# Heads split in the heads loop, gate stores in whole transfers, and a first product between the two second blocks

## The chip, the cores and the metric

The kernel runs on one core of a Trainium2 chip. The metric is the device time of one execution in microseconds, lower being better. Times are medians over runs of the same kernel; the profile is of one execution.

## What is computed

Two "metaformer" stages over x of 32 images, 256 channels, 14 x 14 pixels. This change touches only the last sub-stage, a mixture of experts in which each of the 6272 tokens is cut into 8 heads of 32 values:

```python
h = x @ Wm + bm                       # tokens x 256
t = h.reshape(bs * L_ * H, HD)        # 8 heads of 32
w = jax.nn.softmax(t @ expert_emb, axis=-1)          # 16 experts
topw, topi = jax.lax.top_k(w, 2)
hmid = jax.nn.gelu(jnp.einsum('td,edi->tei', t, W1) + b1, approximate=False)
eo = jnp.einsum('tei,eio->teo', hmid, W2) + b2
comb = (take_along_axis(eo, topi) * topw[:, :, None]).sum(axis=1)
out = comb.reshape(bs, L_, d) @ Wo + bo              # added to the residual
```

The kernel computes all 16 experts for every head and weighs them with gates that are zero but for the top two.

## The kernel before

The program is a row of blocks; in each the five engines run their own instruction streams and meet at semaphores. Two blocks matter.

**The heads loop** (`T` = 16 chunks of `CH` = 392 tokens). Per chunk GpSimd gathers expert rows of an earlier stage (8 indirect DMAs, L1748), VectorE and ScalarE weigh them, normalise, squeeze and excite, and five steps after a chunk's weighing ScalarE's `heads` (L1909) writes the heads of the chunk into `hs`, a two-deep buffer. SP stores them to `hs_d` (L1715), and the exponentials of the gate logits to `ex_d` (L1717). `heads` waits until the store two chunks back has landed. The gates of a chunk ("route", 16 small VectorE steps, `route`, L1599 to L1622) need four transposes on TensorE (L1635), a copy to `wts` on VectorE (`route_copy`, L1643) and stores to `wt_d` on SP (`route_store`, L1649). Chunks 0 and 1 are routed at the end of the heads loop; the other 14 inside the expert loop. A store is one DMA for each of the 8 heads and each piece of the chunk that falls into one column of 256 tokens: 16 or 24 DMAs.

**The expert loop** runs over 49 units of 1024 columns (4 heads of 256 tokens; the last 8 heads of 128). SP loads a unit's heads four times, one below the other, into `stk` (L2158). GpSimd's `split` writes them as fp32r into `x_r` (L2206) and puts into rows 64 to 127 what the rounding lost (L2208). A unit is four slots, one for each group of four experts; the loop has 201 slots. In slot k TensorE does

- `first(4k+e)` for e = 0 to 3 (L2233): w1 times the unit, two matmuls of 512 columns into one of three `psA` buffers. It waits for the GELU three products back.
- after e=2, `second(k-1, b)` for b = 0 and 1 (L2243): w2 of four experts side by side on the columns of the array, into `psY`, which has two buffers.
- after e=0 the extras of the slot: `fold` (L2254, in slots 4w+6) adds up the four experts of a unit; `last` (L2264, in slots 8c+11 and 8c+12) is the output product; `route_pe` (L1635, 14 slots).

ScalarE does nothing but the GELU of each first product (L2292). VectorE runs in the same fixed order: the fold's copy (L2322), the output's sum (L2329), the copy to `wts`, then the two weighings with the gates (L2313), then the slot's route steps, if any. GpSimd adds the weighed groups (L2222). SP, in order, in slot k: the heads of the next unit every fourth slot, the exponentials of a later route, the gate stores, the gates of group k+2 (L2168, four DMAs of 128 KB, one for each expert, into one of three `wb` buffers), the output.

## Time and profile before

| | us |
|---|---|
| median of 3 runs (lowest, highest) | 2449.26 (2446.92, 2452.71) |
| the profiled execution, its own time | 2452.87 |
| its span on the chip | 2451.2 |

| engine | busy us | share |
|---|---|---|
| TensorE, matmuls | 2084.4 | 85% |
| VectorE | 1347.7 | 55% |
| ScalarE | 1289.6 | 53% |
| GpSimd | 968.5 | 40% |

The shares are means over blocks with different limits. The page names lines of the kernel (L2292) with the tiles they write and read; "[0.33 <-PE psA]" behind an instruction is the time for which its engine sat idle before it and what ended that.

### The profile page before, as it was taken

The page shows a single profiled execution, that of the slowest core. Times are in us where ns is not written, and L with a number is a line of the kernel's source. Part 1 is how long each engine was busy: PE and PEld are TensorE (multiplying, and loading weights), DVE is VectorE, ACT ScalarE, POOL GpSimd, SP SyncE. Part 2 cuts the span into 40 slices and gives each one's busy share as a digit, 9 for nine tenths or more (in the row PEclk, how much of TensorE's full clock was granted, in tenths as well). Part 3 has the DMA queues.
Part 4 walks back from the last instruction along what each step waited for, and adds up shares of the span by engine and source line. Part 5 has one row for each costly group of instructions (what it writes and reads, how often), then busy time and mean ns, then how long its engine had stood idle before and what let it go on. Part 6 is the DMA issues. An engine that isn't in the chain of part 4 may idle for free. (4 is left out here: it accounts for less than half of the span.)

```text
span 2451.2 us, 36445 instructions
## 1 busy us (share of the span) xinstructions
PE 2084.4 (85%) x12850; PEld 1158.6 (47%) x12851; DVE 1347.7 (55%) x2117; ACT 1289.6 (53%) x1634; POOL 968.5 (40%) x673
## 2 busy tenths in 40 slices
PE   6998599997977864775799964999999999999998
PEld 3444355554535544664466542444444444444444
DVE  5666435554458861221566652676666666666633
ACT  2444222222544421111344423888888888898887
POOL 4332111210004772001775002655565656565554
PEclk8999779998897757998698886999999999999999
DMA  2110212210724434555232104556565656565563
GB/s 54 28 33 8 86 46 68 65 64 34 250 62 126 145 98 129 172 172 158 72 106 93 48 33 104 141 143 156 147 172 146 156 149 160 148 159 145 146 157 107
DMA packets 206933, 274.84 MB, mean 112 GB/s; under 512 B 49190, under 2 KB 163446, under 8 KB 206646
## 3 DMA queue, kind: packets, MB, share of 16 engines
q1 hardware_dynamic: 173366, 227.84, 33.6%
q0 software_dynamic: 12288, 25.72, 3.5%
q10 hardware_dynamic: 21120, 19.18, 2.3%
q8 instruction: 98, 1.61, 0.3%
q14 instruction: 61, 0.50, 0.1%
HBM read 203.76 MB, written 68.83 MB: 111 GB/s over the span
## 5 line engine op out<-in xcount | busy, mean ns | idle before, releaser
L2292 ACT ACTIVATE BIG<-psA,b_s 128x1024 f32<-128x1024 f32 x784 | 809.8, 1115 | 127.8 <-PE psA L2233 127.5
L2233 PE MATMUL psA<-x_r,w_r 128*128 128x512 f32 x1568 | 477.9, 427 | 46.8 <-ACT BIG L2292 24.9
L2222 POOL TENSOR_TENSOR BIG<-BIG 128x1024 f32<-128x1024 f32 x147 | 376.6, 2562 | 356.4 <-DVE BIG L2313 222.6
L2313 DVE SCALAR_TENSOR_TENSOR BIG<-psY,b_s,BIG 128x512 f32<-128x512 f32 x392 | 292.1, 750 | 340.4 <-PE psY L2243 261.6
L2233 PEld LDWEIGHTS psA<-x_r,w_r 128*128 128x128 f32 x1568 | 269.3, 190 | 314.5 <-ACT BIG L2292 220.9
L2243 PE MATMUL psY<-BIG,w_s 128*32 128x512 f32 x3136 | 388.0, 607 | 15.9 <-DVE BIG L2313 8.2
L2243 PEld LDWEIGHTS psY<-BIG,w_s 128*32 128x32 f32 x3136 | 80.1, 109 | 214.8 <-issue 132.2
L715 DVE TENSOR_REDUCE b_nm<-psN 112x32 f32<-112x512 f32 x128 | 83.1, 686 | 152.9 <-PE psN L612 152.5
L1191 POOL DMA_INDIRECT xg_d<-xnb,SLOT x128 | 135.0, 1055 | 80.4 <-DVE SLOT L1306 43.9
L1524 PE MATMUL ps<-BIG,xv 128*128 x528 | 132.4, 394 | 39.2 <-ACT xv L1535 29.5
L1748 POOL DMA_INDIRECT gath<-yg_d,SLOT x128 | 137.2, 1072 | 65.8 <-issue 36.9
L553 POOL CAST b_pat_r<-BIG 72x3584 fp32r<-72x3584 f32 x16 | 50.7, 3170 | 224.8 <-PE psN L612 211.9
L1535 ACT ACTIVATE xv<-ps 128x512 f32<-128x512 f32 x66 | 39.4, 597 | 188.9 <-PE ps L1513 188.9
L715 DVE TENSOR_REDUCE a_nm<-psN 98x32 f32<-98x512 f32 x128 | 82.4, 685 | 89.0 <-PE psN L603 88.9
L1524 PEld LDWEIGHTS ps<-BIG,xv 128*128 128x128 f32 x528 | 95.8, 191 | 65.0 <-issue 54.5
L2206 POOL CAST x_r<-xv 128x1024 fp32r<-128x1024 f32 x49 | 51.9, 1059 | 186.8 <-DMA xv<-hs_d 186.6
L2208 POOL TENSOR_TENSOR x_r<-xv,x_r 64x1024 fp32r<-64x1024 f32 x49 | 118.0, 2407 | 3.9
L576 PE MATMUL ps<-BIG,b_wb 72*128 72x392 f32 x256 | 100.6, 539 | 3.5 <-DVE xv L721 3.5
L771 ACT ACTIVATE b_exs<-ps 128x1568 f32<-128x1568 f32 x32 | 47.3, 1477 | 104.3 <-PE ps L581 104.3
L1733 POOL MEMSET embd<- 128x64 f32 x1 | 0.2, 156 | 211.9 <-POOLq L1496 211.9
L612 PE MATMUL psN<-b_wb_r,b_pat_r 73*112 73x128 f32 x512 | 71.1, 286 | 14.8 <-POOL b_pat_r L553 14.0
L612 PEld LDWEIGHTS psN<-b_wb_r,b_pat_r 73*112 73x112 f32 x512 | 61.5, 194 | 35.6 <-POOL b_pat_r L553 14.8
(394 smaller groups left out, 3266.3 us busy)
## 6 DMA issues: line engine op xcount, KB each, us to landing
BIG<-wt_d SPq DMA_DIRECT2D x784, 128.0 KB, 2.8
xv<-hs_d SPq DMA_DIRECT2D x196, 128.0 KB, 3.0
BIG<-ypad_d SPq DMA_DIRECT2D x144, 120.0 KB
xg_d<-ex SPq DMA_DIRECT2D x64, 264.0 KB, 3.8
xv<-xg_d SPq DMA_DIRECT2D x66, 256.0 KB, 2.9
xv<-x SPq DMA_DIRECT2D x64, 196.0 KB, 2.7
yg_d<-ex ACTq DMA_DIRECT2D x33, 256.0 KB, 3.2
yg_d<-sq ACTq DMA_DIRECT2D x33, 256.0 KB, 3.2
```

Source lines behind the costliest of these rows:

```text
L576: eng.matmul(ps4[:, i, 0:CH], w_, src, start=True, stop=False)
L612: mm = eng.matmul(psN[0:SR, bank, g * 128:(g + 1) * 128], pat_r[0:KR, bank * 4 + g, sub * SR:(sub + 1) * SR], wb_r[0:KR, bank * 4 + g], st ...
L715: eng.tensor_reduce(dst, src, AX.X, ALU.max, negate=True).then_inc(S["max"], 1)
L1191: eng.indirect_dma_start(xg_d.ap(), bass.IndirectOffsetOnAxis(ap=SLOT[:, t * NSUB + s, j:j + 1], axis=0), xnb[:, t % XB, s], None).then_in ...
L1524: m = eng.matmul(psZ[:, u, r * C:(r + 1) * C], xt[:, u, r, h * 128:(h + 1) * 128], w_moe_s[:, bass.ds(e * (2 * C) + h * C, C)], start=(h = ...
L1748: eng.indirect_dma_start(gath[:, c % GB, 2 * s + j], None, yg_d.ap(), bass.IndirectOffsetOnAxis(ap=SLOT[:, c * NSUB + s, j:j + 1], axis=0) ...
L2208: eng.tensor_tensor(x_r[64:128, w % 2], stk[64:128, w % 2], x_r[64:128, w % 2].bitcast(F32), ALU.subtract).then_inc(Q["lo"], 1)
L2222: eng.tensor_tensor(gacc[:, w % 2], gacc[:, w % 2], gsum[:, a % 2], ALU.add).then_inc(Q["acc"], 1)
L2233: mm = eng.matmul(psA[m % 3][:, b * BLK:(b + 1) * BLK], w1_r[:, m % 16], x_r[:, w % 2, b * BLK:(b + 1) * BLK], start=True, stop=True)
L2243: mm = eng.matmul(psY[use % 2][32 * e:32 * e + 32, :], w2_s[:, g % 4 * 4 + e], hid[:, (4 * g + e) % 8, b * BLK:(b + 1) * BLK], start=True, ...
L2292: eng.activation(hid[:, m % 8], psA[m % 3][:], ACT.Gelu, bias=b1_s[:, m % 16:m % 16 + 1]).then_inc(Q["gel"], 1)
L2313: eng.scalar_tensor_tensor(out=dst, in0=psY[use % 2][:], scalar=b2_s[:, g % 4:g % 4 + 1], in1=wb[:, g % 3, b * BLK:(b + 1) * BLK], op0=ALU ...
```

## The change

Four things change.

1. GpSimd splits the heads in the heads loop, once per chunk and eight chunks behind the gathers: into `hs_r`, in the memory of `xs`. SP stores both parts, two DMAs per chunk, into `hs_d`, now of two planes. In the expert loop SP loads both straight into `x_r`; `split` and `stk` are gone.
2. `wt_d` is laid out as column, head, expert, token instead of expert, column, head, token. A gate store is then one DMA of all 128 rows for each piece: 2 or 3 of them. A gates load reads 4 heads of one expert, 16 KB apart, in pieces of 1 KB instead of 4 KB in one.
3. `fold` moves from behind e=0 to just before the second blocks, and is last of the extras in order.
4. In slots whose extras are none or a fold alone, the second block b=1 follows first product e=3 instead of standing behind b=0.

```diff
-                for h in range(NH):
-                    eng.dma_start(wt_d.ap()[:, c, h, at_:at_ + n], wts[h * NE:(h + 1) * NE, off:off + n]).then_inc(q_wst, 16)
+                eng.dma_start(wt_d.ap()[c].rearrange("h e n -> (h e) n")[:, at_:at_ + n], wts[:, off:off + n]).then_inc(q_wst, 16)
...
-        hs_d = nc.dram_tensor("hs_d", [C, T * CH], F32)
-        wt_d = nc.dram_tensor("wt_d", [NE, -(-(T * CH) // 256), NH, 256], F32)
+        hs_d = nc.dram_tensor("hs_d", [2, C, T * CH], F32)
+        wt_d = nc.dram_tensor("wt_d", [-(-(T * CH) // 256), NH, NE, 256], F32)
...
-                    wait(eng, H["hs"], c + 1)
-                    eng.dma_start(hs_d.ap().rearrange("(h p) (t c) -> t p h c", h=2, t=T)[c], hs[:, c % 2]).then_inc(f_hst[c % 2], 16)
+                    wait(eng, H["lo"], c + 1)
+                    for i in range(2):
+                        eng.dma_start(hs_d.ap()[i].rearrange("(h p) (t c) -> t p h c", h=2, t=T)[c], hs_r[:, i].bitcast(F32)).then_inc(f_hst, 16)
...
+                def split(c):
+                    wait(eng, H["hs"], c + 1)
+
+                    wait(eng, f_hst, c * 32)
+                    eng.tensor_copy(hs_r[:, 0], hs[:, c % 2]).then_inc(H["hi"], 1)
+                    wait(eng, H["hi"], c + 1)
+                    eng.tensor_tensor(hs_r[:, 1], hs[:, c % 2], hs_r[:, 0].bitcast(F32), ALU.subtract).then_inc(H["lo"], 1)
+
+                LEAD = 8
+                for c in range(T + LEAD):
+                    if live(c):
+                        gather(c)
+                    if live(c - LEAD):
+                        split(c - LEAD)
...
                 def heads(c):
-                    wait(eng, f_hst[c % 2], c // 2 * 16)
+                    wait(eng, H["lo"], c - 1)
...
-            EXTRAS[k] = [kind for kind, table in (("fold", FOLD), ("last", LAST), ("route", ROUTE)) if k in table]
+            EXTRAS[k] = [kind for kind, table in (("last", LAST), ("route", ROUTE), ("fold", FOLD)) if k in table]
...
         def heads_load(eng, w):
-            wait(eng, Q["lo"], w - 1)
+            wait(eng, Q["mm1"], 16 * (w - 1))
             tok, n, head, heads = UNITS[w]
             for r in range(4):
-                eng.dma_start(stk[32 * r:32 * r + 32, w % 2, 0:heads * n].rearrange("p (q c) -> p q c", q=heads),
-                              hs_d.ap()[32 * head:32 * (head + heads), tok:tok + n].rearrange(
+                eng.dma_start(x_r[32 * r:32 * r + 32, w % 2, 0:heads * n].bitcast(F32).rearrange("p (q c) -> p q c", q=heads),
+                              hs_d.ap()[r // 2, 32 * head:32 * (head + heads), tok:tok + n].rearrange(
                                   "(q p) c -> p q c", q=heads)).then_inc(q_stk[w % 2], 16)
...
-                src = wt_d.ap()[g % 4 * 4 + e, tok // UT, head:head + heads, 0:n]
+                src = wt_d.ap()[tok // UT, head:head + heads, g % 4 * 4 + e, 0:n]
...
                         if k < NG:
                             first(4 * k + e)
-                        if e == 0 and "fold" in EXTRAS[k]:
-                            fold(FOLD[k], EXTRA_USE["fold", k])
                         if e == 0 and "last" in EXTRAS[k]:
                             last(*LAST[k], EXTRA_USE["last", k])
                         if e == 0 and "route" in EXTRAS[k]:
                             route_pe(eng, ROUTE[k], EXTRA_USE["route", k])
-                        if e == 2 and 0 < k <= NG:
-                            for b in range(NB):
+                        if e == 2 and "fold" in EXTRAS[k]:
+                            fold(FOLD[k], EXTRA_USE["fold", k])
+                        for b in range(NB if 0 < k <= NG else 0):
+                            if e == (2 + b if EXTRAS[k] in ([], ["fold"]) else 2):
                                 second(k - 1, b)
```

## Rows read from the trace of the kernel before

**Rows 1.** Busy time by engine in the expert loop: PE, PEld, DVE, ACT, POOL, clock, DMA.
```profile
1510.00:2440.00 930.00, 889.34 (x5319) 397.77 (x5318) 573.80 (x723) 809.45 (x784) 537.58 (x242) 0.99 0.57 150
```

**Rows 2.** ScalarE's timeline: start us, us, GELUs of one slot, idle before them.
```profile
1569.43 4.13 ACT L2292 ACTIVATE BIG<-psA,b_s 128x1024 f32<-128x1024 f32 x4 [1.70 <-PE psA L2233]
1573.89 4.13 ACT L2292 ACTIVATE BIG<-psA,b_s 128x1024 f32<-128x1024 f32 x4 [0.34 <-PE psA L2233]
1578.62 4.13 ACT L2292 ACTIVATE BIG<-psA,b_s 128x1024 f32<-128x1024 f32 x4 [0.60 <-PE psA L2233]
```

**Rows 3.** Timeline, TensorE in slots without an extra: start us, us.
```profile
1966.44 0.73 PE L2233 MATMUL psA<-x_r,w_r 128*128 128x512 f32 x2 [0.27 <-ACT BIG L2292]
1967.10 1.92 PE L2243 MATMUL psY<-BIG,w_s 128*32 128x512 f32 x16
1967.56 0.13 PEld L2243 LDWEIGHTS psY<-BIG,w_s 128*32 128x32 f32 x4 [0.30 <-ACT BIG L2292]
1967.99 0.13 PEld L2243 LDWEIGHTS psY<-BIG,w_s 128*32 128x32 f32 x4 [0.30 <-issue]
1968.96 1.67 PE L2233 MATMUL psA<-x_r,w_r 128*128 128x512 f32 x6
```

**Rows 4.** Timeline, TensorE in a slot with an output product.
```profile
2433.65 1.20 PE L2233 MATMUL psA<-x_r,w_r 128*128 128x512 f32 x4
2434.69 1.02 PE L2264 MATMUL psY<-ex,wo_s 128*128 128x256 f32 x4
2435.37 1.28 PE L2233 MATMUL psA<-x_r,w_r 128*128 128x512 f32 x4
2436.58 1.92 PE L2243 MATMUL psY<-BIG,w_s 128*32 128x512 f32 x16
```

**Rows 5.** Timeline, a gate store of 24 DMAs and what follows.
```profile
1645.10 11.25 SPq L1649 DMA_DIRECT2D wt_d<-wts  x24
1656.45 1.76 SPq L2168 DMA_DIRECT2D BIG<-wt_d  x4
1665.77 3.12 ACT L2292 ACTIVATE BIG<-psA,b_s 128x1024 f32<-128x1024 f32 x3 [3.65 <-PE psA L2233]
```

**Rows 6.** Timeline, from the heads loop into the expert loop.
```profile
1479.80 20.25 SPq L1649 DMA_DIRECT2D wt_d<-wts  x40
1486.32 0.92 PE L1635 MATMUL ps<-ident,BIG 98*128 98x98 f32 x4 [9.02 <-DVE BIG L1622]
1488.22 0.57 DVE L1643 COPY wts<-ps 128x392 f32<-128x392 f32 x1 [1.96 <-DMA wt_d<-wts]
1501.50 1.75 SPq L2158 DMA_DIRECT2D xv<-hs_d  x4
1510.37 7.14 ACT L2292 ACTIVATE BIG<-psA,b_s 128x1024 f32<-128x1024 f32 x7 [7.58 <-PE psA L2233]
1512.60 0.50 PEld L2233 LDWEIGHTS psA<-x_r,w_r 128*128 128x128 f32 x2 [0.43 <-DMA wo_s<-wo]
```

**Rows 7.** DMA issues of the whole program: KB each, median us to landing.
```profile
BIG<-wt_d SPq DMA_DIRECT2D x784, 128.0 KB, 2.8
xv<-hs_d SPq DMA_DIRECT2D x196, 128.0 KB, 3.0
```

**Rows 8.** Single lines in the expert loop: duration ns min/median/max, first and last start.
```profile
L1606 DVE TENSOR_TENSOR rt<-rt,rev x28: 674/682/2864, 1531.5 to 2299.8; 98x512 f32<-98x512 f32 x28
L2206 POOL CAST x_r<-xv x49: 1026/1037/1500, 1505.6 to 2410.7; 128x1024 fp32r<-128x1024 f32 x49
L2208 POOL TENSOR_TENSOR x_r<-xv,x_r x49: 2336/2386/2843, 1506.7 to 2411.8; 64x1024 fp32r<-64x1024 f32 x49
```

**Rows 9.** Timeline of the heads loop: VectorE, GpSimd and TensorE around a chunk's gathers.
```profile
1321.31 1.66 DVE L1757 SCALAR_TENSOR_TENSOR yn<-gath,P,yn 98x256 f32<-98x256 f32 x4
1323.81 0.96 POOL L1748 DMA_INDIRECT gath<-yg_d,SLOT  x1 [4.06 <-DVE yn L1757]
1324.21 0.79 PEld L1965 LDWEIGHTS psN<-ident,yn 98*128 98x128 f32 x8
```

More of the change, by code:

```diff
@@ L1064, in build @@
         yg_d = nc.dram_tensor("yg_d", [TILES * ROWS, C], F32)
-        Q = {k: sem(f"q_{k}") for k in ("w", "wo", "set", "hi", "lo", "mm1", "gel", "put", "got", "acc", "rt")}
+        Q = {k: sem(f"q_{k}") for k in ("w", "wo", "set", "hi", "mm1", "gel", "put", "got", "acc", "rt")}
         q_wst = sem("q_wst")
@@ L1579, in stored_gates @@
         def stored_gates(r):
-            return 16 * NH * sum(len(s) for s in GATE_STORES[:r])
+            return 16 * sum(len(s) for s in GATE_STORES[:r])
         def gates_ps(use):
@@ L1647, in route_store @@
             for c, at_, off, n in GATE_STORES[r]:
-                for h in range(NH):
-                    eng.dma_start(wt_d.ap()[:, c, h, at_:at_ + n], wts[h * NE:(h + 1) * NE, off:off + n]).then_inc(q_wst, 16)
+                eng.dma_start(wt_d.ap()[c].rearrange("h e n -> (h e) n")[:, at_:at_ + n], wts[:, off:off + n]).then_inc(q_wst, 16)
         H = {k: sem(f"h_{k}") for k in ("w", "set", "scl", "w0", "y", "tr", "x2", "mean1", "dev1", "sq1", "var1", "log1", "rstd1", "n1",
                                         "ys", "gate", "max", "gexp", "hid", "div", "gtr", "gt", "bc", "mul", "w2", "sgx", "sig", "x3",
-                                        "mean2", "dev2", "sq2", "var2", "log2", "rstd2", "n2", "lin", "hs", "lgd", "mx", "dl", "exp")}
+                                        "mean2", "dev2", "sq2", "var2", "log2", "rstd2", "n2", "lin", "hs", "hi", "lo", "lgd", "mx", "dl", "exp")}
         GB = 3
         h_g = [sem(f"h_g{b}") for b in range(GB)]
-        f_hst = [sem(f"f_hst{u}") for u in range(2)]
+        f_hst = sem("f_hst")
         f_wst = [sem(f"f_wst{u}") for u in range(2)]
-        hs_d = nc.dram_tensor("hs_d", [C, T * CH], F32)
-        wt_d = nc.dram_tensor("wt_d", [NE, -(-(T * CH) // 256), NH, 256], F32)
+        hs_d = nc.dram_tensor("hs_d", [2, C, T * CH], F32)
+        wt_d = nc.dram_tensor("wt_d", [-(-(T * CH) // 256), NH, NE, 256], F32)
         ex_d = nc.dram_tensor("ex_d", [T, SUB, NSUB * NH * NE], F32)
@@ L1683, in build @@
         hs = BIG[:, 2 * T * CH:2 * T * CH + 4 * CH].rearrange("p (u h c) -> p u h c", u=2, h=2)
+        hs_r = xs.bitcast(F32R)
         sq2, rs2 = ex, at[:, 0]
@@ L1724, in _ @@
                         route_store(eng, 0, 0)
+                eng.wait_ge(f_hst, T * 32)
                 for u in range(2):
-                    eng.wait_ge(f_hst[u], T // 2 * 16)
                     eng.wait_ge(f_wst[u], T // 2 * 16)
@@ L1742, in _, with gather @@
                                       base=-32 * r, pattern=[[-1, HD]], channel_multiplier=1).then_inc(Q["set"], 1)
-                for c in range(T):
+                def gather(c):
                     wait(eng, H["w0"], c - GB + 1)
@@ L2095, in build @@
         fin = BIG[:, 30 * BLK:30 * BLK + 2 * UT].rearrange("p (a c) -> p a c", a=2)
-        stk = xv[:].rearrange("p a u h c -> p (a u h c)")[:, 0:4 * BLK].rearrange("p (a c) -> p a c", a=2)
         comb = ex[:].rearrange("p h c -> p (h c)")[:, 0:2 * UT].rearrange("p (a c) -> p a c", a=2)
@@ L2200, in _ @@
             def _(eng):
-                def split(w):
-                    wait(eng, q_stk[w % 2], (w // 2 + 1) * 64)
-                    wait(eng, Q["mm1"], 16 * (w - 1))
-                    eng.tensor_copy(x_r[:, w % 2], stk[:, w % 2]).then_inc(Q["hi"], 1)
-                    wait(eng, Q["hi"], w + 4)
-                    eng.tensor_tensor(x_r[64:128, w % 2], stk[64:128, w % 2], x_r[64:128, w % 2].bitcast(F32),
-                                      ALU.subtract).then_inc(Q["lo"], 1)
-                    wait(eng, Q["lo"], w + 1)
-                split(0)
                 for w in range(NU):
-                    if w + 1 < NU:
-                        split(w + 1)
                     for g in range(1, 4):
@@ L2228, in first @@
                     if m % 16 == 0:
-                        wait(eng, Q["lo"], w + 1)
+                        wait(eng, q_stk[w % 2], (w // 2 + 1) * 64)
                     wait(eng, Q["gel"], m - 2)
@@ L2332, in _ @@
                 for k in range(SLOTS):
-                    if "fold" in EXTRAS[k]:
-                        combine(FOLD[k], EXTRA_USE["fold", k])
                     if "last" in EXTRAS[k]:
@@ L2338, in _ @@
                         route_copy(eng, ROUTE[k], EXTRA_USE["route", k])
+                    if "fold" in EXTRAS[k]:
+                        combine(FOLD[k], EXTRA_USE["fold", k])
                     for b in range(NB if 0 < k <= NG else 0):
```

## The prediction

> **What bounds the kernel now.** I read the page first: its chain of work that ended last goes back only to the start of the last block, the expert loop. So the busy times of that stretch came next [rows 1]. It is 930 us of 2451, with TensorE busy for 889 us, ScalarE for 809, VectorE for 574, GpSimd for 538 and the DMA engines for 57% of it, at a granted clock of 0.99. The stage is 809 us of GELU plus ScalarE's idle time, so each microsecond of that idle time that goes is a microsecond of the whole.
>
> ScalarE's own timeline says where it idles [rows 2]. Four GELUs take 4.13 us, and ahead of the last one of each slot there is one gap: 0.33 us in slots without an extra (such a slot lasts 4.46 us), 0.55 to 1.0 with a fold (48 slots, mean 0.67), about 0.65 with an output product (4.78 us), and 1.70 in every sixth output slot (seven in all). Four slots show 3.3 to 3.8 us.
>
> The small gaps come from TensorE's order [rows 3]. After the first product e=2 stand both second blocks, 1.86 us; only then comes e=3, for which ScalarE is already waiting. In the slot without extra TensorE itself idles 0.27 us, for a GELU, ahead of e=2. In the output slot [rows 4] TensorE's parts add up to the slot itself, 4.78 us: there its work is the bound.
>
> The large gaps come from SP's queue [rows 5]: 24 gate stores hold it for 11.25 us, the gates loads behind them start at 1656.45, and ScalarE stands still for 3.65 us before 1665.77.
>
> Last the seam ahead of the loop [rows 6]. 40 gate stores occupy SP for 20.25 us, to 1500.05, although the last gates are in `wts` at 1488.8. The loads of the heads start at 1501.50, GpSimd splits them, and the first GELU starts at 1510.37, after 7.58 us of waiting for TensorE.
>
> **Gate stores.** Each store issue costs SP about 0.5 us (20.25/40; 11.25/24 = 0.47). Ahead of the loop 40 become 5. The two of chunk 0 leave at 1479.8 and have landed long before 1487. Then VectorE's copy is late: the transposes end at 1487.24 [rows 6], the copy (0.57, now held 1.96 us by a store's landing) at 1487.9; three stores end by 1489.3. From SP's last store to the first load of the loop there are now 1.45 us, so this load goes at 1490.75 instead of 1501.50: **-10.7 us**. In the loop 16 or 24 issues become 2 or 3, and the queue is held for 1.4 us at most. The four large gaps (slots 32, 80, 128, 152; the first is in rows 5) shrink to 0.33: 14.4-1.3 = 13.1 us; three of about 1 us after other stores give 2: **-15 us**.
>
> The new layout makes a gates load 1 KB pieces instead of 4 KB. Heads loads already move 128 KB in 1 KB pieces, in 3.0 us against 2.8 for a 4 KB gates load [rows 7]. Gates have two slots of lead and DMA is busy 57%, so I take 0. The bounds are 0 and, were each group's load in the open, 0.2 x 196 = 39 us.
>
> **Split moved into the heads loop.** In the loop it removes a cast and a subtraction of GpSimd, 1.04 and 2.39 us [rows 8], per unit; only the first pair lies open, 3.5 us after the landing. TensorE could start that much sooner, but its second slot waits for `wo_s`, which lands at 1512.6 [rows 6] and moves only with the seam. Its product is there 1.1 us later, at 1513.7, and the fifth GELU, now at 1510.37+4x1.03 = 1514.5, starts then: **-0.8 us** (bounds 0 and 3.5). It also ends GpSimd's reads in the slots ahead of each fold: a route step takes up to 2.9 us beside GpSimd's two-input work and 0.68 by itself [rows 8].
>
> In the heads loop each chunk gets a CAST and a subtraction of 784 columns instead of 1024: 1.04 x 784/1024 = 0.8 and 2.39 x 784/1024 = 1.8 us, and one store more (some 0.4 us of an SP that idles most of the time). GpSimd now ends a chunk's gathers at 1319.75 and waits 4.06 us for VectorE [rows 9]; 2.6 us fit. The store's landing, awaited by the next split, is hidden by a whole chunk, and `heads` waits for a split two chunks back. But GpSimd's subtraction would stand beside VectorE's L1757, two inputs from SBUF, at 1321.3. Delayed to the subtraction's end (1322.8) it ends at 1324.4 instead of 1322.97; TensorE wants it from 1324.21: 0.2 to 0.3 us in each of the eight chunks that still gather. Later GpSimd is idle and splits as soon as the heads are there, when nothing long with two inputs runs. The last split ends some 3 us after the last heads, before the `exp` that SP waits for anyway. Bounds 0 and 16 x 1.8 = 29 us; I take **+1 us**, since the cover is seen in the rows.
>
> The Trainium skill ("SBUF — State Buffer", section Who interferes with whom) says that a VectorE instruction with two SBUF inputs and a GpSimd instruction that reads SBUF block each other wholly. The trace agrees: 0.68 to 2.86 us for one and the same step [rows 8]. By this rule the price is the subtraction's full length wherever both meet, 29 us were all of it on the path; that is the upper bound above.
>
> **First product between the second blocks.** TensorE's terms [rows 3]: one matmul of a first product in a row costs (1.67-0.73)/4 = 0.235 us; a first product from a standstill until the next second block 0.66; two second blocks 1.86, which are four turns of 0.43 (weight loads at 1967.56 and 1967.99) and 0.14 until the first product can start. Parted they pay that 0.14 twice: 2.00. (No row has a block between two first products; 0 and the whole 0.43 of another turn are the bounds.) A split slot is then: e=0, 1, 2 in a row 0.66+4x0.235 = 1.60; e=3 alone 0.66; blocks 2.00: **4.26 us** against 4.46. GELU needs 4.13, so TensorE is the bound, and e=3 is ready about 0.5 us ahead of its GELU. A fold beside the blocks adds two turns of half the columns, 0.43: 4.69 against 4.73 to 4.83, mean 4.80, so -0.11. Two output slots of eight keep their order. Their terms now [rows 4]: two first products ahead of the output product 1.04, that 0.68, e=1 and 2 1.21, blocks 1.86, sum 4.79. The first loses its leading e=3 to the slot before (1.04-0.47 = 0.57) and is 4.32; the second stays 4.79; the slot after them runs e=3, 0, 1 and waits for the GELU as now (4.46-0.66-1.86 = 1.94), then 0.66, both parted blocks 2.00 and e=3 0.66, in all 5.26. The three are 14.37 against 4.78+4.78+4.46 = 14.02. Over eight slots: 3 x -0.20, 2 x -0.11, +0.35, which is -0.47. Times 24.5 (-11.5), less seven slots that have a route and stay as they are (1.4): **-10 us**.
>
> What is queued behind: `fold` and its copy stand later in the slot, and the second block b=1 waits for the copy. With a route step of 0.7 us ahead, the copy ends 0.6 us before b=1 is due. The seven gaps of 1.70 stay: there two route steps, one of them long, hold up VectorE before the output's sum.
>
> The Trainium skill ("TensorEngine Tiling (Array Packing)", Key Properties) says that a change of tiling mode drains TensorE; this change makes four such changes a slot out of two. The rows put 0.14 us on the way back to a first product; the rule names no price.
>
> **Sum.** -10.7 - 15 - 0.8 + 1 - 10 = -35.5 us. The profiled execution took 2452.87 us (span 2451.2 and 1.7 around it), 3.6 above the median 2449.26. I take the sum from the median, 2413.8, and say **2413 us**.
>
> **The rivals.**
> A: parting the blocks costs more than 0.14, say 0.25 us. 141 slots are split; 141 x 0.11 = 16: 2429. (Were it 0.14+0.43, another turn lost each time, it would be 61: 2474.) For it: no row shows a block between two first products without a wait near it. Chance 0.15.
> B: the restart is hidden and slots run at the GELU rate, 0.13 less in 141 slots: 2395. Against it: a lone first product takes 0.66 where two in a row take 0.47. Chance 0.15.
> C: VectorE becomes late. The second weighing follows 0.9 us later, the route steps after it, and fold slots wait for the copy 0.5 us in 48 slots: 2437. For it: VectorE runs beside GpSimd's additions in three slots of four. Chance 0.07.
> D: the large gaps come from the stores' landings, not their issues, and stay: 2428. Against it: in rows 5 the gates load follows the last store's issue at once. Chance 0.04.
> E, slower: in the heads loop each split lies on the path, since GpSimd's next gathers start after it and VectorE is blocked by it: 2.65 us a chunk, 16 x 2.65 = 42: 2455. From 36/16 = 2.3 us a chunk on the kernel is slower. The 4.06 us of idle GpSimd speak against it. Chance 0.04.
>
> **How the numbers follow.** The forecast holds 2403 to 2422, chance 0.55. The range takes in A, B and D: 2392 to 2432; outside are C, E, A's far end and the tails. Less than 0.2% (4.9 us, about what a measurement of this kernel tells from no change) needs nearly all gains to fall away at once: same 0.02, slower 0.04, faster 0.94.
>
> **What would show it.** Seam: SP has 5 store issues, and the loop's first heads load starts some 11 us sooner after the last `ex_d` store. Store gaps: no wait of ScalarE above 1.8 us in the loop. Order: slots without extra 4.2 to 4.3 us; at 4.13 it is B, at 4.37 and over A. Heads loop: GpSimd waiting about 1.3 us a chunk instead of 4.06, and no later end. Wrong if the gates loads land later than the weighing wants them, or the clock of the expert loop falls below 0.98.

## The result, and the profile after

The changed kernel takes **2428.87 us** (median of 4 runs, 2427.95 to 2433.28) against 2448.09 for the kernel before, measured beside it (4 runs, 2446.78 to 2452.71): a ratio of 0.992 with a 95% interval of 0.9903 to 0.9936. It is faster by 19 us and inside the range of 2392 to 2432, but 16 us above the forecast of 2413 and outside 2403 to 2422. The profiled execution took 2433.28 us, with a span of 2431.6.

I cut both traces at the same events: the first weighing on ScalarE (L1872 before, L1888 after), the start of the last write of `heads` (L1909, L1925), SP's first load of the expert loop, the first GELU and the start of the last one.

| us | before | after | difference | forecast |
|---|---|---|---|---|
| blocks ahead of the heads loop (not touched) | 1163.3 | 1168.4 | +5.1 | 0 |
| heads loop | 311.8 | 319.5 | **+7.7** | +1 |
| seam: last heads to first load | 26.4 | 15.8 | **-10.6** | -10.7 |
| first load to first GELU | 8.9 | 5.6 | -3.3 | -3.5 |
| first GELU to last GELU | 928.8 | 909.8 | **-19.1** | -22.3 |
| rest | 12.0 | 12.5 | +0.6 | 0 |
| span | 2451.2 | 2431.6 | -19.6 | -35.5 |

The forecasts of the two rows around the first GELU are the sum's -15, -10 and -0.8 (-25.8), of which 3.5 lie ahead of it. Most of what is missing is in the heads loop and ahead of it.

The expert loop in the busy times by window (window, its length, then PE, PEld, DVE, ACT, POOL, granted clock, DMA share, GB/s), which answers [rows 1]:

```profile
1510.00:2420.00 910.00, 892.17 (x5317) 386.84 (x5315) 524.87 (x724) 811.67 (x784) 373.21 (x146) 0.99 0.57 154
```

All 784 GELUs now fit into 910 us. TensorE's timeline answers [rows 3] and [rows 4], one slot below the other:

```profile
1960.92 1.67 PE L2233 MATMUL psA<-x_r,w_r 128*128 128x512 f32 x6
1962.53 1.06 PE L2243 MATMUL psY<-BIG,w_s 128*32 128x512 f32 x8
1963.52 0.73 PE L2233 MATMUL psA<-x_r,w_r 128*128 128x512 f32 x2
1964.18 1.06 PE L2243 MATMUL psY<-BIG,w_s 128*32 128x512 f32 x8
1965.18 1.67 PE L2233 MATMUL psA<-x_r,w_r 128*128 128x512 f32 x6
1966.78 0.64 PE L2254 MATMUL psY<-BIG,fold 128*32 128x256 f32 x8
1967.23 1.04 PE L2243 MATMUL psY<-BIG,w_s 128*32 128x512 f32 x8
1968.20 0.73 PE L2233 MATMUL psA<-x_r,w_r 128*128 128x512 f32 x2
1968.87 1.06 PE L2243 MATMUL psY<-BIG,w_s 128*32 128x512 f32 x8
1969.87 0.73 PE L2233 MATMUL psA<-x_r,w_r 128*128 128x512 f32 x2
```

The slot without an extra runs from 1960.92 to 1965.18, 4.26 us, and the one with a fold from there to 1969.87, 4.69 us. Nothing stands idle in either. ScalarE's timeline answers [rows 2] and [rows 5]. The first row shows the gap of 1.70 that stays; the second is the place of the first large store gap (slot 32), now 16 GELUs without a gap that the view would part:

```profile
1571.92 5.13 ACT L2292 ACTIVATE BIG<-psA,b_s 128x1024 f32<-128x1024 f32 x5 [1.70 <-PE psA L2233]
1655.82 16.89 ACT L2292 ACTIVATE BIG<-psA,b_s 128x1024 f32<-128x1024 f32 x16 [0.56 <-PE psA L2233]
```

SP's timeline of the same store, the timeline of the seam (answers [rows 6]), and the DMA issues (KB each, median us to landing; answer [rows 7]):

```profile
1646.47 1.38 SPq L1648 DMA_DIRECT2D wt_d<-wts  x3
1647.95 1.81 SPq L2183 DMA_DIRECT2D BIG<-wt_d  x4
...
1500.07 0.57 DVE L1643 COPY wts<-ps 128x392 f32<-128x392 f32 x1 [1.01 <-PE ps L1635]
1503.67 1.76 SPq L2173 DMA_DIRECT2D x_r<-hs_d  x4
1509.29 4.13 ACT L2292 ACTIVATE BIG<-psA,b_s 128x1024 f32<-128x1024 f32 x4 [4.33 <-PE psA L2233]
1515.39 2.93 PE L2233 MATMUL psA<-x_r,w_r 128*128 128x512 f32 x6 [3.58 <-DMA wo_s<-wo]
1516.65 2.12 ACT L2292 ACTIVATE BIG<-psA,b_s 128x1024 f32<-128x1024 f32 x2 [3.24 <-PE psA L2233]
...
BIG<-wt_d SPq DMA_DIRECT2D x784, 128.0 KB, 3.2
x_r<-hs_d SPq DMA_DIRECT2D x196, 128.0 KB, 3.5
```

Three store issues hold SP for 1.38 us instead of 11.25. In the kernel before, VectorE's weighing waited 16 times for a gates load (us in total, times, longest, from 1520 to 2430 us); in the changed kernel the same view has no wait of L2313 for a DMA:

```profile
DVE BIG L2313 <- DMA BIG<-wt_d: 57.5, 16, 6.8
```

In the seam the first load goes 3.6 us after VectorE's copy starts. But the four GELUs that now start early are followed by a wait of 3.24 us: TensorE's slot 1 waits for `wo_s`.

The heads loop, in the timeline around one chunk, answers [rows 9]:

```profile
1282.42 4.44 DVE L1773 SCALAR_TENSOR_TENSOR yn<-gath,P,yn 98x256 f32<-98x256 f32 x4
1283.73 0.85 POOL L1756 CAST xv<-BIG 128x784 fp32r<-128x784 f32 x1
1284.67 1.91 POOL L1758 TENSOR_TENSOR xv<-BIG,xv 128x784 fp32r<-128x784 f32 x1
1286.91 0.56 PE L1981 MATMUL psN<-ident,yn 98*128 98x98 f32 x4 [0.96 <-DVE yn L1773]
```

The four weighing instructions take 4.44 us instead of 1.66. The difference, 2.78, is GpSimd's cast and subtraction together (0.85+1.91 = 2.76), and TensorE waits for VectorE. Six of the 16 groups are over 2 us (4.44, 3.84, 2.25, 4.45, 2.24, 2.24), which adds up to the 9.5 us that the loop's rows differ by. Over the whole loop (VectorE's groups by line in the stretch of the heads loop: busy us, mean ns), before and then after:

```profile
L1757 DVE SCALAR_TENSOR_TENSOR yn<-gath,P,yn 98x256 f32<-98x256 f32 x64 | 26.6, 478 | 11.8 <-ACT yn L1872 11.8
```

```profile
L1773 DVE SCALAR_TENSOR_TENSOR yn<-gath,P,yn 98x256 f32<-98x256 f32 x64 | 36.1, 625 | 12.1 <-ACT yn L1888 12.1
```

### The profile page after: what moved, and what is told of

Read it like the earlier page. It is cut to its first block and busy times, and to the rows that moved or that the text cites. A ratio compares the mean times of both kernels' runs of the same rounds, so it can differ in the third digit from the quotient of the medians.

```text
span 2431.6 us, 36080 instructions
## 1 busy us (share of the span) xinstructions
PE 2097.1 (86%) x12850; PEld 1151.0 (47%) x12851; DVE 1312.8 (54%) x2117; ACT 1292.7 (53%) x1634; POOL 847.6 (35%) x607
## 5 line engine op out<-in xcount | busy, mean ns | idle before, releaser
L2233 PE MATMUL psA<-x_r,w_r 128*128 128x512 f32 x1568 | 484.7, 428 | 19.8 <-ACT BIG L2292 8.2
L2313 DVE SCALAR_TENSOR_TENSOR BIG<-psY,b_s,BIG 128x512 f32<-128x512 f32 x392 | 292.9, 750 | 341.7 <-PE psY L2243 341.3
L2243 PE MATMUL psY<-BIG,w_s 128*32 128x512 f32 x3136 | 407.4, 603 | 6.2 <-DVE BIG L2329 5.9
L2243 PEld LDWEIGHTS psY<-BIG,w_s 128*32 128x32 f32 x3136 | 71.8, 108 | 155.5 <-issue 88.8
L1550 DVE COPY ex<-ps 128x512 f32<-128x512 f32 x33 | 22.8, 691 | 95.7 <-PE ps L1524 94.0
L791 ACT ACTIVATE BIG<-psMO 128x196 f32<-128x196 f32 x32 | 10.7, 333 | 109.6 <-PE psMO L636 109.6
```

The costliest lines, as they stand in the source:

```text
L2233: mm = eng.matmul(psA[m % 3][:, b * BLK:(b + 1) * BLK], w1_r[:, m % 16], x_r[:, w % 2, b * BLK:(b + 1) * BLK], start=True, stop=True)
L2243: mm = eng.matmul(psY[use % 2][32 * e:32 * e + 32, :], w2_s[:, g % 4 * 4 + e], hid[:, (4 * g + e) % 8, b * BLK:(b + 1) * BLK], start=True, ...
L2313: eng.scalar_tensor_tensor(out=dst, in0=psY[use % 2][:], scalar=b2_s[:, g % 4:g % 4 + 1], in1=wb[:, g % 3, b * BLK:(b + 1) * BLK], op0=ALU ...
```

## The experiments

All times are medians; "loop" is the stretch from the first to the last GELU. Ratios are to the kernel before, measured beside each of three groups (its medians there: 2451.67, 2450.18 and 2448.32 us), so kernels of different groups are compared by their ratios.

| kernel | us | ratio (95%) | heads loop | loop |
|---|---|---|---|---|
| blocks together | 2444.39 | 0.9971 (0.9953 to 0.9990) | 318.8 | 924.0 |
| stores by head | 2468.28 | 1.0065 (1.0048 to 1.0082) | 319.6 | 935.8 |
| split among the gathers | 2440.88 | 0.9951 (0.9926 to 0.9976) | 332.9 | 909.7 |
| split in the expert loop | 2426.13 | 0.9900 (0.9882 to 0.9918) | 313.1 | 908.9 |
| output weight later | 2426.98 | 0.9908 (0.9891 to 0.9925) | 320.0 | 904.7 |
| no split | 2421.48 | 0.9888 (0.9872 to 0.9903) | 309.4 | 909.1 |
| split off GpSimd | 2439.23 | 0.9958 (0.9944 to 0.9971) | 322.9 | 909.0 |
| changed kernel again | 2431.71 | 0.9922 (0.9908 to 0.9935) | 319.7 | 910.0 |
| split behind the weighing | 2423.35 | 0.9901 (0.9886 to 0.9917) | 316.3 | 910.0 |
| the same, output weight later | 2419.97 | 0.9890 (0.9875 to 0.9905) | 315.6 | 904.6 |
| split in the expert loop, output weight later | 2422.56 | 0.9892 (0.9877 to 0.9908) | 312.3 | 908.1 |
| order alone | 2442.86 | 0.9987 (0.9971 to 1.0003) | 310.9 | 916.7 |

**1. Blocks together.** The changed kernel with one condition changed:

```diff
-                            if e == (2 + b if EXTRAS[k] in ([], ["fold"]) else 2):
+                            if e == 2:
                                 second(k - 1, b)
```

> The changed kernel, with both second blocks behind e=2 in every slot (the fold still right before them); all else as changed. My theory: a split slot lasts 4.25 us and one with both blocks together 4.46, a fold slot 4.7 against 4.8, and the slot after two output slots gives 0.35 back, so the order is worth 0.35 to 0.5 us in eight slots: 8 to 12 us, time 2437 to 2441, slots without extra back at 4.46. Rival: the whole gain of the expert loop (22 us) is the missing store stalls, and the order is worth nothing: 2429. Other rival: the order is worth 20 us or more and something else in the loop lost: 2449.

The loop is 924.0 us against 909.8: parting the blocks is worth 14.3 us here, more than the 10 of the sum. Some 1.3 of it falls in the first three slots; the rest is 1.5 us for each 24 slots (from slot 86 to slot 110 this kernel needs 112.96 us and the changed one 111.42). A part of it is the fold: with its new place directly ahead of both blocks it makes a gap of 0.76 us at ScalarE (at 1819.54), in all 47 fold slots behind the start, where the kernel before had 0.67 on average. That is some 4 us (47 x 0.09) which the kernel before did not pay, so I estimate the parting at about 10 against that kernel. Rival A falls.

**2. Stores by head.** The changed kernel, its layout kept, with one DMA for each head again:

```diff
-                eng.dma_start(wt_d.ap()[c].rearrange("h e n -> (h e) n")[:, at_:at_ + n], wts[:, off:off + n]).then_inc(q_wst, 16)
+                for h in range(NH):
+                    eng.dma_start(wt_d.ap()[c, h, :, at_:at_ + n], wts[h * NE:(h + 1) * NE, off:off + n]).then_inc(q_wst, 16)
```

> The changed kernel with the new layout of the gates and loads in 1 KB pieces, but stored head by head again: 40 store DMAs ahead of the expert loop and 16 or 24 in it. My theory: it is the issues that cost, so the seam grows by 10.6 us, four gaps of ScalarE over 3 us come back and cost 13 to 15 us: 2429 + 24 to 26 = 2453 to 2455. Rival (D): the landing of the stores, or the layout, made the gaps: then only the seam comes back, 2440.

The seam is 12.0 us longer (27.8) where I expected 10.6, and the loop 26.0 us where I expected 13 to 15: the median is 13 us above the upper end of the forecast for this kernel, and above the kernel before. Rival D falls: the layout is the changed kernel's, and SP, which waits for the stores' landing ahead of the gates loads, does so for 0.4 us at most (us in total, times, longest):

```profile
SPq L2184 <- DMA wt_d<-wts: 5.8, 14, 0.4
```

The kernel before waits as little (5.7 us, 14 times, 0.4). Slot 32 in the timeline:

```profile
1666.15 1.80 SPq L2184 DMA_DIRECT2D BIG<-wt_d  x4
1671.27 1.41 DVE L2314 SCALAR_TENSOR_TENSOR BIG<-psY,b_s,BIG 128x512 f32<-128x512 f32 x2 [6.93 <-DMA BIG<-wt_d]
1675.30 1.11 ACT L2293 ACTIVATE BIG<-psA,b_s 128x1024 f32<-128x1024 f32 x1 [3.90 <-PE psA L2234]
1678.27 2.12 ACT L2293 ACTIVATE BIG<-psA,b_s 128x1024 f32<-128x1024 f32 x2 [1.85 <-PE psA L2234]
```

ScalarE stands still for 5.75 us. From SP's issue of the gates to VectorE's use of them it takes 5.12 us; in the kernel before it was 4.16 (the issue at 1656.45 in [rows 5]):

```profile
1660.61 1.41 DVE L2313 SCALAR_TENSOR_TENSOR BIG<-psY,b_s,BIG 128x512 f32<-128x512 f32 x2 [6.70 <-DMA BIG<-wt_d]
```

**3. Order alone.** To see whether that is the price of the order, the kernel before got only the new order of slots:

```diff
-                        if e == 0 and "fold" in EXTRAS[k]:
-                            fold(FOLD[k], EXTRA_USE["fold", k])
...
-                        if e == 2 and 0 < k <= NG:
-                            for b in range(NB):
+                        if e == 2 and "fold" in EXTRAS[k]:
+                            fold(FOLD[k], EXTRA_USE["fold", k])
+                        for b in range(NB if 0 < k <= NG else 0):
+                            if e == (2 + b if EXTRAS[k] in ([], ["fold"]) else 2):
                                 second(k - 1, b)
```

> The kernel before with the new order of slots alone; stores head by head, split in the expert loop. Theory from the two halves measured so far (the changed kernel without whole stores has a GELU stretch of 935.8 us): with 24 stores in a row SyncE issues the gates' loads late, and more slots stall than before, so the order alone brings nothing: GELU stretch 930 to 937 us, time 2449 to 2456 us. Rival (the order's gain of 14.3 us is its own and does not need the stores): 2435 to 2440 us.

My theory fell, and the median, 2442.86, lies between its forecast and the rival's. The loop is 916.7 us, 12.2 shorter than before, with the 24 stores in place; its first GELU, though, comes 1.5 us later behind the first load. The profiled span is 10 us shorter, the median 5.5, and the interval of the ratio takes in 1: by the medians alone the order by itself isn't told from no change, and its worth is read from the loop. Slot 32 again, SP, VectorE and ScalarE:

```profile
1657.00 1.76 SPq L2168 DMA_DIRECT2D BIG<-wt_d  x4
1661.12 1.41 DVE L2313 SCALAR_TENSOR_TENSOR BIG<-psY,b_s,BIG 128x512 f32<-128x512 f32 x2 [5.80 <-DMA BIG<-wt_d]
1663.78 1.11 ACT L2292 ACTIVATE BIG<-psA,b_s 128x1024 f32<-128x1024 f32 x1 [1.41 <-PE psA L2233]
```

The gates are as late as in the kernel before, but ScalarE waits 2.0 us at this place (1.41 and, one GELU later, 0.60) instead of 3.65: with e=3 between the blocks it has one more GELU to do while b=1 waits for VectorE. So order and stores overlap: 12.2 us for the order alone and 26.0 for the stores on top of the changed kernel are not terms of one sum. The kernel of experiment 2 differs from this one also in a later landing (median 3.4 us for a gates load against 2.8) and a longer issue (12.30 us for 24 stores against 11.38). That these two make it so much worse is argued from the rows; no run has them apart. Which of the layout and the second half of `hs_d` brings the later landing stands in the next experiment's DMA rows.

**4. Split in the expert loop.** The kernel before with whole stores, new layout and new order, so the changed kernel less its first part (two of the places, against the changed kernel):

```diff
-                    for i in range(2):
-                        eng.dma_start(hs_d.ap()[i].rearrange("(h p) (t c) -> t p h c", h=2, t=T)[c], hs_r[:, i].bitcast(F32)).then_inc(f_hst, 16)
+                    eng.dma_start(hs_d.ap().rearrange("(h p) (t c) -> t p h c", h=2, t=T)[c], hs[:, c % 2]).then_inc(f_hst[c % 2], 16)
...
+                split(0)
                 for w in range(NU):
+                    if w + 1 < NU:
+                        split(w + 1)
```

> The kernel before with whole gate stores, the new layout and the new order of fold and second blocks, but with the split left on GpSimd in the expert loop and the plain heads stored: the change without its first part. My theory: the moved split cost 7.6 us in the heads loop and gave about nothing at the start of the expert loop (0.8 us worse, by the wait for wo_s), so without it: 2429 - 7 = 2419 to 2423, less if the split's reads slow the route steps ahead of the folds (up to 2 us each in a dozen slots, mostly hidden). Rival: the split's removal from the expert loop is what lets fold slots run at 4.7, and without it the loop is 10 us longer: 2430 or more.

2426.13 us, a ratio of 0.9900, whose interval overlaps those of the changed kernel (0.992 and, in experiment 10, 0.9922). The profiled span, 2423.6, is 8 us under the changed kernel's, 3.3 of it in blocks that the two share. The stages are clearer. The heads loop is 6.4 us shorter without the split. The loop is 908.9 us with the split in it and 909.8 without, but that hides two opposite effects. With the split moved out, the first GELU comes 3.3 us sooner behind the first load, yet slot 3 ends 1.6 us later (27.42 us against 25.78), by the wait for `wo_s`. From there to the last GELU it takes 888.0 us without the split and 892.1 with it. The 4.1 us lie in nine slots with a fold. In each of them a route step takes 2.0 to 2.9 us and TensorE waits behind it; slot 58:

```profile
1769.89 2.37 POOL L2207 TENSOR_TENSOR x_r<-xv,x_r 64x1024 fp32r<-64x1024 f32 x1
1769.96 2.85 DVE L1606 TENSOR_TENSOR rt<-rt,rev 98x512 f32<-98x512 f32 x1
1772.74 0.41 DVE L2321 COPY ex<-psY 128x256 f32<-128x256 f32 x1
1773.30 1.07 PE L2242 MATMUL psY<-BIG,w_s 128*32 128x512 f32 x8 [0.47 <-DVE ex L2321]
1775.11 1.11 ACT L2291 ACTIVATE BIG<-psA,b_s 128x1024 f32<-128x1024 f32 x1 [1.09 <-PE psA L2232]
```

The route step takes 2.85 us beside GpSimd's subtraction, the fold's copy comes late, TensorE waits for it, and ScalarE's gap is 1.09 us where the changed kernel has 0.56. The DMA rows of this kernel:

```profile
BIG<-wt_d SPq DMA_DIRECT2D x784, 128.0 KB, 3.2
xv<-hs_d SPq DMA_DIRECT2D x196, 128.0 KB, 3.4
```

Against [rows 7] both land 0.4 us later, though the heads loads of this kernel are unchanged. The order alone leaves both at 2.8 and 3.0, and stores by head on the new layout have 3.4 and 3.5; so it goes with the layout of `wt_d`, not with the split, the order or the form of the stores.

**5. Output weight later.**

```diff
-                eng.dma_start(wo_s[:], wo.rearrange("(h p) e -> p h e", p=128)).then_inc(Q["wo"], 16)
+                eng.dma_start(wo_s[:], wo.rearrange("(h p) e -> p h e", p=128)).then_inc(q_wo2, 16)
...
-                        eng.wait_ge(Q["wo"], 32)
+                        eng.wait_ge(Q["wo"], 16)
+                    if k == min(LAST):
+                        eng.wait_ge(q_wo2, 16)
```

> The changed kernel, with one edit: the output weight wo_s, whose load stood between TensorE's slot 1 and its data (a wait of 4.3 us at TensorE), gets a semaphore of its own, waited for ahead of the first output product. Theory (the early start of the heads is spent waiting for this load): the loop's start keeps the 3.25 us that its first GELU gained, the stretch from the first to the last GELU is 2 to 3.5 us shorter, 2425 to 2427 us. Rival (slot 1 is set by the gates' landing, which is next in the same queue): within 0.7 us of the changed kernel.

The loop is 904.7 us, 5.1 shorter, where I expected 2 to 3.5, and the median 4.7 under that of the changed kernel in the same group, with intervals that overlap. TensorE's timeline at its start:

```profile
1506.76 6.21 PE L2234 MATMUL psA<-x_r,w_r 128*128 128x512 f32 x14 [7.92 <-DMA x_r<-hs_d]
```

Fourteen matmuls run in a row where the changed kernel stopped after eight. On top of the split left in the expert loop the same edit was not told apart. I had written

> Whole stores and the new order with the split left in the expert loop, and the output weight waited for later. Theory: with the split at the loop's start (8.95 us to the first GELU) the weight is hardly late for slot 1, so its wait gives less here than the 5 us with the changed kernel: 0.5 to 2 us, 2424 to 2426 us. Rival (the weight's transfer lies on the way of the gates' loads and it is the wait as such): 5 us less, 2421 us.

and the profiled spans are the same to 0.1 us (2423.7 and 2423.6); the loop is 0.8 shorter, but its first GELU came 1.6 later, since SP's four first loads took 3.42 us to issue instead of 1.76. The ratios are 0.9892 and 0.9900 with intervals that overlap. Between this kernel and the changed one with the weight later, the split's price in the loop shows again: 891.3 us against 888.0 from slot 3's end.

**6. No split.** The split is left out: GpSimd only gathers in the heads loop, and both halves of `hs_d` are stored from `hs`, so the expert products read the whole head twice.

```diff
-                    if live(c - LEAD):
-                        split(c - LEAD)
...
-                        eng.dma_start(hs_d.ap()[i].rearrange("(h p) (t c) -> t p h c", h=2, t=T)[c], hs_r[:, i].bitcast(F32)).then_inc(f_hst, 16)
+                        eng.dma_start(hs_d.ap()[i].rearrange("(h p) (t c) -> t p h c", h=2, t=T)[c], hs[:, c % 2]).then_inc(f_hst[c % 2], 16)
```

> The changed kernel without the split: in the heads loop GpSimd issues its gathers alone, and the heads as ScalarE wrote them are stored to both halves of hs_d (so the expert products read the whole head twice, and the output is not the reference's). The stores, their count and bytes, are those of the changed kernel. Theory (the two GpSimd instructions slow the VectorE instructions beside them): the heads loop goes from 319.5 us back to 310 to 314 us, and the kernel's time to 2419 to 2424 us. Rival (the second store of each chunk and its waits do it): the heads loop stays at 317 to 321 us.

The heads loop falls by 10.1 us to 309.4, and the weighing group is back to 26.6 us. The second store of each chunk costs nothing. So it is the two GpSimd instructions. Nor is it the waits that came with them: with the split and without, ScalarE idles 0.77 to 0.87 us ahead of `heads` in the first ten chunks, and from the sixth chunk on it starts its weighing without idle time, so the gathers, though they start later, are never late. How much of the 10.1 is clock is told below.

**7. Split among the gathers.** The split moves from behind a chunk's eight gathers to between its third and fourth:

```diff
+                            if 2 * s + j == 3 and live(c - LEAD):
+                                split(c - LEAD)
...
-                    if live(c - LEAD):
+                    elif live(c - LEAD):
                         split(c - LEAD)
```

> The changed kernel with GpSimd's split of a chunk standing between the third and the fourth gather of the next turn instead of behind the eighth (in the turns that still gather); same instructions, same counts. There VectorE runs no instruction with two SBUF inputs for some 3 us. My theory: the split costs the heads loop 7.6 us because VectorE's four L1773 (4.44 us instead of 1.66 in the chunk at 1282) stand behind GpSimd's reads, TensorE waits, and its clock falls to 1.2 GHz. So L1773 is back at 1.66 in nearly all chunks, the heads loop ends 5 to 8 us sooner, time 2421 to 2424. Rival: it is GpSimd's extra 2.8 us a chunk or the second store, wherever they stand: 2429, the heads loop as long as now.

A miss, and in the other direction: I expected 5 to 8 us less, and the heads loop is 13 us longer. The weighing is at 1.66 us again in 12 of the 16 groups, but now the split meets VectorE's small steps:

```profile
1302.07 0.85 POOL L1758 CAST xv<-BIG 128x784 fp32r<-128x784 f32 x1
1303.01 1.84 POOL L1760 TENSOR_TENSOR xv<-BIG,xv 128x784 fp32r<-128x784 f32 x1
1303.25 1.62 DVE L1803 TENSOR_SCALAR gate<-gate,gs 2x8 f32<-2x8 f32 x1
1304.93 0.16 PE L2028 MATMUL ps<-ident,gate 2*8 2x2 f32 x1 [1.44 <-DVE gate L1803]
```

An instruction of 8 columns takes 1.62 us instead of 0.22, and TensorE waits for it at once.

**8. Split behind the weighing.** GpSimd waits for VectorE's weighing, splits, and only then gathers:

```diff
                 for c in range(T + LEAD):
-                    if live(c):
-                        gather(c)
+                    weighed(c)
                     if live(c - LEAD):
                         split(c - LEAD)
+                    if live(c):
+                        gather(c)
```

> The changed kernel with the heads split at another place of GpSimd's order: ahead of a chunk's eight gathers, right behind the wait for VectorE's weighing of an earlier chunk, instead of behind the gathers. There VectorE has no weighing to do, and two of its next instructions read PSUM. Theory (what stands beside the split sets its price): no group of four weighing instructions over 2 us while gathers run, heads loop 310 to 315 us instead of 319.5, time 2422 to 2427 us. Rival (the gathers now start 2.9 us later in each chunk, and the weighing waits for them; or the subtraction falls beside VectorE's small steps for the gate, as in the kernel with the split among the gathers): 322 to 333 us.

The heads loop is 316.3 us, 3.2 shorter and 1.3 above what I expected; the ratio is 0.9901 where the changed kernel had 0.9922 in the group before, about 5 us, with intervals that overlap (0.9886 to 0.9917 and 0.9908 to 0.9935). One chunk:

```profile
1279.16 1.66 DVE L1776 SCALAR_TENSOR_TENSOR yn<-gath,P,yn 98x256 f32<-98x256 f32 x4
1280.94 0.84 POOL L1758 CAST xv<-BIG 128x784 fp32r<-128x784 f32 x1 [1.86 <-DVE yn L1776]
1281.86 1.85 POOL L1760 TENSOR_TENSOR xv<-BIG,xv 128x784 fp32r<-128x784 f32 x1
1282.54 0.97 DVE L1828 TENSOR_TENSOR xv<-V,psMO 128x784 f32<-128x784 f32 x1
```

The weighing is at its old length (one group of the 16 is over 2 us, at 2.25), and beside the subtraction VectorE runs L1828, whose other input is in PSUM, in its old 0.97 us.

With the output weight later as well:

> The same with the output weight on its own semaphore, waited for ahead of the first output product (which took 5 us out of the loop in an earlier run). Theory: the two add, 5 us less than the kernel with the split behind the weighing, 2417 to 2422 us, and the shortest of all kernels here. Rival: the gathers suffer, 2427 us or more.

The two add in the stages (315.6 and 904.6 us), and 2419.97 us is the shortest median here. Against the changed kernel the intervals just meet (0.9905 and 0.9903), against its second measurement they don't (0.9908); from the two kernels with the split in the expert loop it isn't told apart.

**9. Split off GpSimd.** ScalarE writes the rounded half from PSUM, VectorE subtracts behind `choose`:

```diff
+                    for m_ in range(2):
+                        m = eng.activation(hs_r[:, 0, m_], ps4[:, m_, 0:CH], ACT.Identity, bias=bm_s[:, m_:m_ + 1])
+                    m.then_inc(H["hi"], 1)
...
+                def split(c):
+                    wait(eng, H["hi"], c + 1)
+                    eng.tensor_tensor(hs_r[:, 1], hs[:, c % 2], hs_r[:, 0].bitcast(F32), ALU.subtract).then_inc(H["lo"], 1)
```

> The changed kernel with the same split on other engines: ScalarE writes the rounded half from PSUM (two more activations a chunk, about 1.06 us), VectorE subtracts behind choose (one more instruction a chunk, about 0.96 us); GpSimd only issues gathers. Theory (it is GpSimd's sharing with VectorE that costs, not the work as such): the heads loop is shorter than the changed kernel's 319.5 us if the extra VectorE microsecond of each chunk finds VectorE idle, 312 to 317 us, and no group of four weighing instructions takes over 2 us. Rival (VectorE is the bound of the loop, so its microsecond lies on the path): 16 chunks by 0.96 us over the 311.8 of before, 325 to 328 us.

No weighing group is slow, yet the heads loop takes 322.9 us, near the rival's 325 to 328. So an added microsecond of VectorE doesn't hide either, or the one added to ScalarE; this kernel has both and doesn't tell them apart.

**10. The changed kernel again.**

> The changed kernel once more, unchanged, for what two executions of one program differ by, stage by stage. Theory: heads loop 317 to 322 us, GELU stretch 909 to 911 us, the stages ahead of the heads loop 1161 to 1169 us (they differ by some microseconds from run to run), time 2426 to 2431 us. Rival: the heads loop's 7.6 us are of one execution's clock and do not come again (310 to 314 us).

Heads loop 319.7 us and loop 910.0: both come again (eight weighing groups are over 2 us, where the first profile had six). The blocks ahead of the heads loop took 1166.1. Over all the kernels here, which share these blocks, they took 1159.7 to 1168.4 us.

**What a chunk costs.** A chunk's time depends on the granted clock too. Busy times by window, one chunk each, before in the first fence, after in the second (columns as above):

```profile
1276.50:1290.90 14.40, 13.10 (x71) 8.77 (x70) 10.62 (x23) 7.75 (x19) 8.21 (x8) 1.00 0.37 114
1290.90:1306.90 16.00, 14.70 (x71) 9.65 (x71) 10.64 (x23) 7.76 (x19) 8.52 (x8) 0.89 0.29 89
1321.30:1340.50 19.20, 17.90 (x71) 11.56 (x70) 10.61 (x23) 7.69 (x19) 8.84 (x8) 0.73 0.24 75
```

```profile
1267.30:1282.40 15.10, 13.18 (x71) 8.78 (x70) 11.59 (x23) 7.75 (x19) 12.44 (x11) 1.00 0.40 126
1282.40:1299.40 17.00, 14.76 (x71) 9.35 (x70) 13.35 (x24) 7.91 (x19) 13.41 (x12) 0.90 0.40 126
1330.30:1350.40 20.10, 17.86 (x71) 11.61 (x71) 13.33 (x23) 7.88 (x19) 14.56 (x13) 0.75 0.37 116
```

TensorE is busy for 13.1 of 14.4 us: the heads loop is TensorE's, with 1.3 us of slack a chunk. At a like clock a chunk with a collision is 0.7 to 1.0 us longer, with VectorE at 11.6 to 13.4 us instead of 10.6. From the sixth chunk to the last but one the kernel before takes 157.2 us and the changed one 165.2. About 3.1 of the 8.0 are such excesses at a like clock. The other 4.9 are that three chunks ran at 0.73 to 0.75 where before it were two; each costs 4.8 us over one at 1.00, the level of 2.4 GHz. In the second profile of the changed kernel the slow chunks stand elsewhere (0.74, 0.68, 0.73), and the heads loop is as long (319.7 us). It is no chance of one execution: the five profiles with the split behind the gathers have heads loops of 318.8 to 320.0 us, the five with no split there 309.4 to 313.1. The kernel without a split has a single chunk at 0.73, so a good part of its 10.1 us is clock as well. How a chunk's short waits of TensorE for VectorE bring on a low clock some chunks later these runs don't settle.

## Why the prediction was right or wrong

**Seam: right.** -10.6 against -10.7. That it fits to 0.1 us is luck: VectorE's last copy came 12.2 us behind the last heads instead of 12.8, and the load 3.6 us behind the copy's start instead of 2.85.

**Store gaps: right in kind, too high in size.** The four large gaps went, and the longest wait of ScalarE behind the start is 1.71 us. D is refuted by the changed kernel and experiment 2: the issues block, not the landings, and a queue that is late costs more than I had counted. From slot 30 to 38, 78 to 86, 126 to 134 and 150 to 158 the changed kernel gains 3.8, 3.8, 3.6 and 3.3 us, in sum 14.4. But the order by itself (experiment 3) already gains 6.6 there, and with the blocks together (experiment 1) it is 11.7. So the stores are worth 7.8 us in these places on top of the order and up to 11.7 without it, against the 13.1 of the sum.

**Order: right, to the hundredth where it was worked out.** Slots of 4.26 and 4.69 us stand in the trace as they stand in the sum; the three slots from 1969.87 to 1984.57 take 14.70 against 14.37, with a route in the second that takes 0.36 more than the sum's output slot. A and B fall, and so does C: the fold slot takes 4.69 us, not 0.5 more. What the order is worth depends on the neighbour: 12.2 us alone, and the parting of the blocks alone 14.3 in the changed kernel.

**The two together: 23.1 us from slot 3's end on, where I had 25, and the closeness is partly luck.** The steps between the kernels are 11.1 us for the order (911.1 us in the kernel before, 900.0 in experiment 3), 7.9 for the whole stores with their layout (892.1 in experiment 4) and 4.1 for the split moved out (888.0). The sum had 10, 15 and nothing.

**DMA pieces: right.** Loads land 0.4 us later, and with two slots of lead the weighing never waits for them in the changed kernel. With SP late they may be part of the 26 us of experiment 2, which no run shows apart.

**Loop start: the size was off.** Slot 3 ends 0.8 us later, measured from the first load, instead of 0.8 sooner. I let the fifth GELU follow the landing of `wo_s` by a product's length; it does start behind the landing (the weight releases TensorE 11.7 us behind the first load, 11.1 before), but then slot 1 still has three first products and its blocks ahead of it, which the kernel before had done by that time. The wait itself could go: 5 us.

**Heads loop: the failing step.** "It ends at 1324.4 instead of 1322.97 ... 0.2 to 0.3 us in each of the eight chunks". I took GpSimd's 4.06 us of idle time [rows 9] as cover. But the row says what it waits for: VectorE's weighing. GpSimd is idle just ahead of VectorE's two-input work and during it, so work put there meets it. The weighing then waits for the cast too, not for the subtraction alone: up to 2.79 us, not 1.4, and 0.6 where it meets only the end of the subtraction. Six groups of sixteen are slow, and smaller steps with them (L1810, 1.19 us instead of 0.16, at 1271.47). That gives VectorE 14 us more in the loop (203.15 us busy in 320 against 189.17 in 312). TensorE's slack absorbs most of it; with the clock's part it comes to +7.7, against +1, inside the bounds of 0 to 29. Rival E had half of the mechanism, VectorE blocked by the split, with 2.65 us a chunk where 0.5 was measured; its other half, the later gathers, is not on the path (experiment 6). GpSimd's wait is 2.31 us where I said 1.3 (at 1320.06), and "no later end" was wrong. The Trainium skill ("SBUF — State Buffer", section Who interferes with whom) lists `tensor_scalar` beside instructions with two SBUF inputs as one that can take the shared ports. Experiment 7 agrees, with its 1.62 us for 8 columns. I had applied the rule to L1757 alone.

**Blocks not touched: +5.1.** No step of mine. They spread by 8.7 us over programs that share them, so 5 us of any single pair of profiles says nothing.

**What removing the split was to bring** had two parts: cheaper route steps and an earlier start. To the first the prediction gave no term, though it had read the price of a step in [rows 8]. The step takes at most 0.69 us now (L1606; [rows 8] had 2.86), and with it the slots of experiment 4 gain 4.1 us. The second was lost at `wo_s`. On balance the change's first part as it stands costs about 4 us in the stages that it touches (heads loop +6.4, seam +0.2, first load to last GELU -2.5): without it the kernel takes 2426.13 us, which the medians don't tell apart. With the split behind the weighing and the weight later the same stages are 4.9 us shorter than with the split left in and the weight later (+3.3, +0.2, -8.4); there, too, the medians (2419.97 and 2422.56) don't tell them apart.

**The range.** It reached to 2432 for the sake of A, B and D, and none of the three came true. That it holds 2428.87 is luck: what fills it is the heads loop (6.7 us off), the blocks not touched (5.1) and the loop (3.2).

## What to carry to other kernels

Before you fill an engine's idle time, read what that wait is for: where it is another engine's work that shares ports with the new one, the gap is a bad place, and just behind it a better one (319.5 and 316.3 us here, and 332.9 at a third place among small steps). An early start is worth only what the next wait leaves, so follow the first slots to the second and third wait. Where two totals agree, cut them at one more event: 908.9 and 909.8 us hid a loss of 1.6 us and 3.3 of early start on one side and a gain of 4.1 on the other. And two edits to one late queue don't add: measure each alone and on top of the other.

## What was not expected of the hardware

- A VectorE instruction with 8 columns took 1.62 us beside GpSimd's subtraction, 0.22 by itself; four weighing instructions waited for a cast and a subtraction in full (4.44 us, and 1.66+0.85+1.91 is 4.42).
- A chunk with the same instructions took 14.4 us at a granted clock of 1.00, 16.0 at 0.89 and 19.2 at 0.73.
- Loads whose own form was unchanged landed 0.4 us later when others came in 1 KB pieces.
